# A copy of half a megabyte from DRAM to DRAM at every fourth step of a two-layer graph kernel

## The reference, cut to what matters

```python
# layer 0: h = relu(layernorm(x))
agg = jnp.zeros_like(x).at[row].add(edge_attr)          # row = src: 100000 rows of 256 floats
h = jnp.concatenate([x, agg, x_with_cond], axis=1)
h = jax.nn.relu(h @ W1.T + b1)
x = x + h @ W2.T + b2
# layer 1: h = relu(layernorm(x))
ht = jax.nn.relu(h @ W1 + b1)
msg = jax.nn.sigmoid(w * ht[src] + b_param)             # a row gathered for every edge
fsum = jax.ops.segment_sum(msg, dst, num_segments=6250)
c = (jnp.log(s / (1.0 - s)) - b_param) / w              # s = clip(fsum)
bundle = jnp.concatenate([ht, c], axis=1) @ Wn + bn
out = x + jax.nn.relu(bundle / norm)                    # norm over the features
```

## Time and profile before

| | us |
|---|---|
| median of three runs | 2870.13 |
| the profiled execution's own time | 2868.22 |
| its span in the trace | 2866.5 |
| first loop, stretch read here | 437 to 1356 |
| second loop, stretch read here | 1576 to 2727 |

### The profile page before, as it was taken

The page is one execution under the profiler, slowest core; times in us unless marked ns, Lnnn a source line. Parts: engine busy times, 40 slices in busy tenths (PEclk is TensorE's granted clock), DMA queues, the critical chain, the costliest instruction groups (busy, mean ns, idle before and its releaser), DMA issues.

```text
span 2866.5 us, 34135 instructions
## 1 busy us (share of the span) xinstructions
PE 2071.8 (72%) x8433; PEld 1340.2 (47%) x8433; DVE 1914.2 (67%) x5018; ACT 1304.0 (45%) x4298; POOL 1746.8 (61%) x1674
## 2 busy tenths in 40 slices
PE   1489856667767776867997576877787786786784
PEld 0356633434434443534786353544543453454453
DVE  1578844765776875777786487577677677653378
ACT  0245423435534633634436243553563463374465
POOL 1568877767676666665015666667666666666503
PEclk9789967878888987989998688888898898898798
DMA  9989868435533333332447333333333333334434
GB/s 381 252 179 209 170 104 242 113 91 137 129 93 88 92 91 89 90 92 73 154 149 261 93 96 91 102 98 92 103 99 91 104 97 90 97 119 122 121 117 162
DMA packets 182549, 370.71 MB, mean 129 GB/s; under 512 B 33244, under 2 KB 101622, under 8 KB 179781
## 3 DMA queue, kind: packets, MB, share of 16 engines
q0 software_dynamic: 93168, 219.39, 30.6%
q1 hardware_dynamic: 77991, 114.14, 12.4%
q10 hardware_dynamic: 11200, 35.00, 3.2%
HBM read 281.76 MB, written 99.74 MB: 133 GB/s over the span
## 4 chain that ended last, share of the span: by engine, by line
PE 39%; DVE 22%; issue 18%; another core or an unknown queue 10%; ACT 3%; SPq 3%; DMA 2%; POOL 1%; DVEq 1%; ACTq 0%; POOLq 0%
PE bank L1474 37%; DVE agg L1229 9%; DVE hits L1156 2%; DVE oh L1160 1%; SPq L476 1%; DVE store L1160 1%; DVEq L1221 1%; ACT oh L832 1%; DVE store L1410 1%; DVE hit L1152 1%; DVE cum L1113 1%; POOL agg_copy L666 1%; ACT dist L824 1%; POOL store L692 1%
## 5 line engine op out<-in xcount | busy, mean ns | idle before, releaser
L1474 PE MATMUL bank<-store,oh 128*128 (+2 forms) x4610 | 1352.3, 427 | 463.1 <-DVE agg L1229 167.9
L1474 PEld LDWEIGHTS bank<-store,oh 128*128 128x128 f32 (+1 forms) x4610 | 809.0, 196 | 899.8 <-issue 450.9
L1229 DVE TENSOR_TENSOR agg<-bank,agg 128x256 f32 x1845 | 773.9, 419 | 506.8 <-PE bank L1474 253.0
L692 POOL DMA_INDIRECT store<-g_table,idx_all x785 | 769.2, 980 | 387.1 <-issue 179.5
L832 ACT ACTIVATE oh<-dist 128x128 f32<-128x128 f32 x1845 | 498.3, 301 | 1051.7 <-PE bank L1474 620.0
L692 POOL DMA_INDIRECT store<-in_edge_attr,idx_all x628 | 623.1, 992 | 284.9 <-issue 146.2
L824 ACT ACTIVATE dist<-iota,nloc_all 128x128 f32<-128x128 f32 x1845 | 582.8, 386 | 73.1 <-DVE nloc_all L1201 42.2
L666 POOL DMA_INDIRECT agg_copy<-agg x160 | 263.7, 1648 | 152.2 <-ACT agg L789 57.7
L1474 PE MATMUL bank<-oh,hit 125*128 125x314 f16 x720 | 154.6, 343 | 47.7 <-DVE oh L1160 36.8
L1156 DVE TENSOR_TENSOR hits<-iota,ttab 125x628 f16<-125x628 f16 x360 | 171.4, 476 | 0.0
L1160 DVE TENSOR_TENSOR oh<-hits,v 125x628 f16<-125x628 f16 x360 | 166.2, 479 | 3.2
(11 more groups left out here) (206 smaller groups left out, 1852.2 us busy)
## 6 DMA issues: line engine op xcount, KB each, us to landing
agg_copy<-store ACTq DMA_DIRECT2D x4, 6400.0 KB
agg<-in_edge_attr SPq DMA_DIRECT2D x39, 512.0 KB
agg_copy<-agg_copy POOLq DMA_DIRECT2D x16, 800.0 KB
store<-g_table,idx_all POOLq DMA_INDIRECT x785
store<-in_x SPq DMA_DIRECT2D x48, 256.0 KB
store<-in_edge_attr,idx_all POOLq DMA_INDIRECT x628
pre_scratch<-store SPq DMA_DIRECT2D x25, 256.0 KB
agg<-agg_copy SPq DMA_DIRECT2D x25, 256.0 KB
```

The lines of the kernel that those rows point to most:

```text
L692: gp.indirect_dma_start(out=store[:, at % RING * D:(at % RING + 1) * D], out_offset=None, in_=table_dram, in_offset=bass.IndirectOffsetOnA ...
L1229: dve.tensor_tensor(to, pt[n % TB][:, 0:D], to, ALU.add).wait_op(s_mm, n + 1, "sem-ge").then_inc(s_acc, 1)
L1474: return pe.matmul(o, l, r, start=start, stop=stop, skip_group_check=skip)
```

## The change

In both loops SyncE gets a new instruction at each step t with t % 4 == 1, which is 39 a group and 351 in all: `spin(g, t)` waits until all jobs ahead of job (g, t) are done, waits for the landing of the spin before it, and then issues a DMA from the first 512 rows of the input `edge_attr` (1 KB each) to a new DRAM tensor of the same size. In the built program it stands as 16 rows of 8192 floats, 32 KB each. Nothing reads the copy. In the first loop the column starts of sorts 1 to 4 now stand at their steps among the spins, and behind the wait for `s_a1`, which stood behind them; in the second loop the spins stand between the loads, the stores and the column starts that were there. At the very end SyncE also waits for the last spin.

```diff
@@ -155,6 +155,7 @@
+        spin_dram = nc.dram_tensor("spin_scratch", (2 * P, 2 * D), F32).ap()
@@ -356,6 +357,7 @@
+        s_spin = sem("s_spincopy")
@@ -546,9 +548,22 @@
-            for sig in range(1, G1 + 1):
-                column_starts(sig)
+            spins = itertools.count()
+
+            def spin(g, t):
+                n = next(spins)
+                sp.wait_ge(s_mm, NTH[g, t])
+                if n:
+                    sp.wait_ge(s_spin, 16 * n)
+                sp.dma_start(spin_dram, a["edge_attr"][0:4 * P, :].rearrange("(p j) f -> p (j f)", j=2)).then_inc(s_spin, 16)
+
             sp.wait_ge(s_a1, 2 + NW)
+            for g in STAGES[0]:
+                for t in range(TILES):
+                    if PLACE_ATOM + 3 in atoms_at(0, g, t):
+                        column_starts(g + 1)
+                    if t % TB == 1:
+                        spin(g, t)
             sp.wait_ge(s_mm, JOBS1)
@@ -630,6 +647,7 @@
             sp.wait_ge(s_fs, 16 * NW)
+            sp.wait_ge(s_spin, 16 * next(spins))
```

## The result

The changed kernel takes 2919.55 us (median of 4 runs, 2911.89 to 2922.32); the kernel before took 2871.72 us beside it (4 runs, 2869.02 to 2876.31). The ratio is 1.0157, with a 95% interval of 1.0141 to 1.0172: 48 us slower, where the forecast was 2873 us and the range ended at 2905.

What follows compares the result with a forecast made beforehand. The loops were taken as paced by the ring product, add, one-hot, product, not by data. Gathers 0, column starts 2.5 and chunks 1.5 us gave 4 us, partly hidden, so +3 us and 2873 us; range 2864 to 2905.

Steps and rivals of the forecast that it cites:

- Length of a copy, and the DMA share: Both loops: a copy takes 3.8 us, bounds 2.9 to 5.8; DMA share rises from about 0.32 to 0.55 to 0.68.
- SyncE keeps up under the tipping point: SyncE's queue in both loops: copies under 5.9 us cost SyncE nothing; above it every load behind is late.
- a spin has landed when the next falls due: SyncE's queue: at 3.8 us a copy, with 5.9 us between copies, SyncE is idle a third of the time.
- Gathers: GpSimd's gathers in both loops: doubled DMA share costs them 0 us; other end 114 us.
- Chunk loads: Second loop: loads mostly come after the copy ahead has landed; 0.1 us each, 1.5 us, high end 50 us.
- Column starts: Eight column starts near or behind copies: 2.5 us in all, low end 0, high end 17 us.
- The reading of sort 2: Column starts beside an 800 KB add: the small store waits for nearly the whole add, loaded after 7.4 us instead of 1.5.
- Chunk stores: Second loop: stores land later, ScalarE waits 3 to 5 us at some 15 copies but catches up; 0 us.
- cover gone: Chunk stores' high end without ScalarE's one-hots up to 12 jobs ahead of TensorE: 15 x 4 = 60 us.
- rival 1: Moderate lateness: half of 32 exposed DMAs late by 1.37 us, 22 us, giving 2892 us; chance 0.20.
- fewer adds in every stretch alike: Sign in the loops that the forecast is wrong: the copy reaches something held untouched; forecast expected 73 to 77 adds in 56 us.
- the high ends of chunks: Left out of the range, second loop: 50 us for late chunk loads, 60 us for late stores without cover.

Runs made afterwards that it cites:

- e4: Changed kernel with each copy 1 KB instead of 512 KB, same order and waits; 1.0004 times the kernel before on chip 8.
- e1: Changed kernel with each chunk store of the second loop right behind a load, all 351 copies kept; 1.0031 times the kernel before on chip 8.
- e2: Changed kernel with the column starts of sort 1 ahead of all copies, all 351 copies kept; 1.0014 times the kernel before on chip 8.
- d1: Changed kernel with early chunk stores, sort 1's column starts first, and copies of 1 MB; 1.1404 times the kernel before on chip 12.
- e3_both_again: Changed kernel with chunk stores right behind loads and sort 1's column starts ahead of all copies; 1.0006 times the kernel before on chip 12.
- p2b: Changed kernel with early chunk stores and sort 1's column starts first, no copies, only SyncE's job-counter waits; 1.0001 times the kernel before on chip 15.
- e3_both_third: Changed kernel with chunk stores right behind loads and sort 1's column starts ahead of all copies; 1.0090 times the kernel before on chip 6.
- p1: Changed kernel without its copies, keeping SyncE's waits on the job counter; 0.9992 times the kernel before on chip 12.

## Why the prediction was wrong, step by step

Three steps failed: the column starts were priced at 1 us at sort 1 and came 20.2 us late; the chunk stores were priced at 0 and made ScalarE wait up to 14.6 us; and the number of DMAs had no term and costs 18 to 25 us on chips of the first kind.

- **Length of a copy, and the DMA share: right.** 3.8 us taken, 3.58 measured (bounds 2.9 to 5.8); shares of 0.65 and 0.60 in the forecast's 0.55 to 0.68. The three sizes here (3.58, 4.46 and 5.55 us, each on another chip) lie within 0.11 us of a line of 1.6 us plus 1.97 us for each half megabyte, and the copies of 1 KB in e4 take 1.68 us. The estimate by the Trainium skill (DMA: Bandwidth & Descriptors, Anatomy of one DMA) was 3.2 us. The page gives its two parts for DMAs that GpSimd issues and counts the handling of completion; these copies are SyncE's, and SyncE goes on after 3.89 us.
- **SyncE keeps up under the tipping point: right in the mean, not copy by copy.** Half a megabyte stays under it, 1 MB goes over it and costs 14%. But "a spin has landed when the next falls due" held for 235 of 350 copies only; the prediction set the landing against the mean distance of 5.9 us and not against the shortest.
- **Gathers: right, as far as shown.** 0 us for the bytes beside them, and 15.5 and 3.9 us of waits.
- **Chunk loads: right, as far as shown.** 12.4 and 5.2 us of waits against 12.8 and 8.1.
- **Column starts: the step that failed first.** I priced each as if one copy stood ahead of it, 1 us at sort 1 and 17 us for all eight at the high end. I had not asked what is due at the moment when SyncE comes free of the fills: five copies stand in a row, and the first four take 27.6 us to land. The column starts came 20.2 us later than before, and one wait was 24.0 us, more than my high end for all eight together. On chip 8 the columns alone, e1, cost 8.1 us.
- **The reading of sort 2 under it: wrong in the mechanism.** I let the small store "wait for nearly the whole add" and worked out from the Trainium skill (DMA: Bandwidth & Descriptors, Queues, rings and completion order) that by turns it would land in little over 1.5 us. The packets of the trace show turns: the store is 98 pieces of 320 B, and they move from 714.55 to 719.03 between the add's 128 pieces of 6400 B, of about 0.50 us each. On 16 engines that is six or seven small pieces each behind one of eight large ones, some 3 us and more by this estimate. So turns and a long landing go together.
- **Chunk stores: the step that failed second.** I moved a store by "about three steps" and looked at group 8, where chunks are six steps apart. In groups 4 to 7 the store of the product at step 147 goes to step 8 of the next group, while the next chunk's copy comes at step 155, and the double jobs there use up the one-hots made ahead twice as fast. I gave the cover at its full length of 12 jobs and took 0; the high end I wrote for "cover gone" was 60 us. The 60 us of ScalarE's waiting were near the 73.6 measured; but they came in fewer and longer pieces, up to 14.6 us, and those reach TensorE. On chip 8 the stores alone, e2, cost 3.7 us. Together both cost 22 us on chip 6, which is the sum of rival 1 (22 us: 2892). That the numbers agree is luck: rival 1 counted 16 transfers late by 1.37 us each, and here it is one by 20.2 us and a few stores.
- **What had no term: the number of DMAs.** 18 to 25 us on chips of the first kind, the largest single part of the loss there (25 of 47 us on chip 6). The prediction counted only what a copy's bytes and its place in the queue do. By what path it costs stays open. It named the sign of this case, "fewer adds in every stretch alike"; in 56 us such a loss is 0.5 to 0.7 of an add and can't be seen.
- **The range.** It left out "the high ends of chunks"; by the runs on chip 6 the 48 us are two lateness terms and this third one together, each with the same sign. The chance of 0.60 for the forecast rested on hidden costs being zero one by one.

## What to carry to other kernels

Tying a queue's instructions to the steps of a loop changes when everything behind them goes out: walk the whole queue, the group boundaries and the moment when the queue comes free first, and count how many of the new instructions are due by then. Here bytes beside a loop that had DMA share to spare cost nothing that could be told as long as the copies landed within four steps on the mean; past that point, in d1, the lag went to every transfer behind. A view that counts waits must be read with the order in which the queue waits: 329 waits stood in a kernel that lost nothing, 337 in one that lost 368 us. A loss of under one per cent without a wait of its own needs runs that take bytes, DMAs and waits away one by one, and on more than one chip, since slack differs from chip to chip.

## What was not expected of the hardware

**Two kinds of chips.** The same kernel takes 2624 to 2632 us on chips 8 and 12 and 2872 to 2894 us on the first chip, 6 and 15: 9 to 10%. Instructions have the same lengths (a one-hot 0.30 us, a gather's issue 0.98 us on both). What differs are the signals of TensorE. On the quick chips the job counter goes up 14 ns after the end of a product (median), and 1 of 1836 increments in e3_both_again comes more than 0.5 us after it; on the first kind the median is 15 ns, but 367 of 1479 in the kernel before come later than that, one in ten by more than 2.2 us. The kernel's other engines wait for that counter, and moments of over 1 us in which no engine of the core works are there 28 to 44 times in the loops (44 to 70 us in all), and at most twice on the quick chips (d1 apart). From p2b on chip 15:

```profile
1718.36 0.69 PE L1490 MATMUL bank<-store,oh 128*128 x2 [0.18 <-issue]
...
1719.92 0.31 ACT L848 ACTIVATE oh<-dist 128x128 f32<-128x128 f32 x1 [1.81 <-PE bank L1490]
...
1723.44 0.43 DVE L1168 TENSOR_TENSOR hit<-iota,rtab 125x512 f16<-125x512 f16 x1 [5.21 <-remote]
...
1724.72 0.50 PEld L1490 LDWEIGHTS bank<-store,oh 128*128 128x128 f32 x2 [6.07 <-ACT oh L848]
```

and the granted clock around it (the third number from the end):

```profile
1716.00:1718.00 2.00, 1.44 (x8) 0.69 (x6) 1.36 (x4) 0.51 (x2) 1.39 (x3) 1.00 0.32 102
...
1720.00:1724.00 4.00, 0.00 (x0) 0.00 (x0) 0.56 (x2) 1.86 (x8) 1.29 (x3) 0.73 0.24 71
...
1724.00:1728.00 4.00, 3.27 (x9) 2.32 (x10) 4.00 (x12) 1.78 (x8) 3.09 (x4) 0.50 0.23 68
```

The products end at 1719.05 by the trace; the counter goes up at 1719.90, 1723.46, 1723.50 and 1723.60, and ScalarE, GpSimd and VectorE start with it. TensorE ran at 2.4 GHz (1.00), did nothing for over 4 us, and came back at 1.2 GHz (0.50). Such a late increment is what stands as "remote" in the waits: the profile finds no product that ended shortly before it. No wait on "remote" is in the traces of the quick chips. The mean granted clock is 0.89 to 0.90 in the profiled executions there (but for d1, 0.85) and 0.85 to 0.86 on the first kind. What makes the increments late isn't shown: whether a product really ends later than the trace has it, or its signal is held up. Nor is it shown whether the recording has a part in it: the first kind's traces also lack most increments of landings (1410 to 1832 of 5616 are there, on the quick chips 5503 to 5615), and each copy adds 16 of them. It is a rival for the cost of the 351 DMAs that no run tests.

**A small transfer beside large ones.** The 31 KB of column starts took from 480.46 to 488.07 to be stored at sort 1 in the changed kernel, about as long as the 7.4 us at sort 2 before the change, but by another way. At sort 2 their pieces moved in turns with those of an add. At sort 1 the fifth copy stood on the same queue, issued 0.54 us earlier; the first small piece moved at 485.88, when the copy's last one was about to end (485.98). Where neither stood just ahead of it, the same store took 2.3 us (e3_both_third), 2.6 (before), 3.1 (e2) and 3.8 (p1).
